# Three images of a conv-and-attention kernel: the cast after gelu set ahead of the exponentials, two low halves side by side, and input differences earlier

## What is computed

```python
perceived = conv_general_dilated(x, w_perc, padding='SAME', feature_group_count=Cc) + b_perc
hid = gelu(einsum('bphw,dp->bdhw', perceived, w_up1) + b_up1)
dx = einsum('bdhw,cd->bchw', hid, w_up2) + b_up2
h_new = transpose(x + dx)
qkv = einsum('bhwc,dc->bhwd', h_new, w_qkv) + b_qkv
scores = stack([(q * kp[shifted by dy, dx]).sum(-1) for dy, dx in _POS]) * scale
out = sum(softmax(scores)[i] * vp[shifted by dy, dx] for i in range(9))
return h_new + out
```

## Time and profile before

| what | value |
|---|---|
| median of 3 runs | 404.14 us (403.94 to 404.82) |
| the profiled execution's own time | 405.43 us |
| its span, first to last instruction | 403.1 us |
| TensorE busy | 386.1 us (96%) |
| TensorE weight loads | 362.9 us (90%) |
| VectorE busy | 340.5 us (84%) |
| ScalarE busy | 320.6 us (80%) |
| GpSimd busy | 177.4 us (44%) |
| mean granted TensorE clock | 0.990 |

### The profile page before, as it was taken

How to read it: one execution, slowest core, us unless ns; L and a number is a source line. 1 busy time by engine, 2 the same in 40 slices (tenths; PEclk the granted TensorE clock), 3 DMA queues, 4 the chain that set the end, 5 groups by cost and what they waited for, 6 DMA issues and landing times.

```text
span 403.1 us, 10500 instructions
## 1 busy us (share of the span) xinstructions
PE 386.1 (96%) x3674; PEld 362.9 (90%) x3674; DVE 340.5 (84%) x922; ACT 320.6 (80%) x710; POOL 177.4 (44%) x156
## 2 busy tenths in 40 slices
PE   6999975999999999999999999999999999999994
PEld 5999964998999999999999999999999999999874
DVE  5999975798898888888898888889888888886785
ACT  7635568789797997979798897979799797978873
POOL 6785164362626354351636354351636345032110
PEclk9999996999999999999999999999999999999999
DMA  7420300204013050504013050503104030301003
GB/s 232 167 65 2 120 0 18 101 2 146 28 55 116 2 172 1 169 0 131 38 34 135 0 169 0 169 0 104 65 12 157 0 104 2 104 2 54 3 37 120
DMA packets 11513, 28.57 MB, mean 71 GB/s; under 512 B 2400, under 2 KB 3296, under 8 KB 11488
## 3 DMA queue, kind: packets, MB, share of 16 engines
q1 hardware_dynamic: 11200, 28.21, 20.6%
q10 hardware_dynamic: 288, 0.05, 0.1%
HBM read 19.86 MB, written 8.39 MB: 70 GB/s over the span
## 4 chain that ended last, share of the span: by engine, by line
PE 73%; DVE 4%; issue 1%; POOL 0%; DVEq 0%; ACT 0%
PE m_ps L469 39%; PE s_ps L594 8%; PE work L524 8%; PE work L568 6%; PE s_ps L577 5%; PE s_ps L563 2%; PE s_ps L560 1%; PE s_ps L561 1%; PE work L594 1%; DVE t L946 1%; PE work L547 0%; DVE o_sb L1120 0%; PE m_ps L606 0%; DVE ptc L1111 0%; DVE pt L1126 0%
## 5 line engine op out<-in xcount | busy, mean ns | idle before, releaser
L469 PE MATMUL m_ps<-thi,whi 128*128 128x256 f32 x558 | 159.7, 286 | 0.7 <-DVE ru_sb L1034 0.4
L469 PE MATMUL m_ps<-thi,wlo 128*128 128x256 f32 x558 | 156.2, 280 | 0.0
L469 PE MATMUL m_ps<-tlo,whi 128*128 128x256 f32 x558 | 155.0, 278 | 0.0
L469 PEld LDWEIGHTS m_ps<-thi,whi 128*128 128x128 f32 x558 | 105.7, 189 | 4.0 <-issue 1.0
L469 PEld LDWEIGHTS m_ps<-tlo,whi 128*128 128x128 f32 x558 | 106.5, 191 | 0.7
L469 PEld LDWEIGHTS m_ps<-thi,wlo 128*128 128x128 f32 x558 | 105.6, 189 | 0.0
L1345 POOL TENSOR_TENSOR hid_lo<-hid,hid_hi 128x1024 fp32r<-128x1024 f32 x30 | 72.4, 2412 | 24.9 <-ACT hid_hi L726 20.4
L781 ACT COPY pt<-ptc 32x256 f32<-32x256 f32 (+3 forms) x186 | 73.0, 393 | 5.5 <-DVE ptc L1111 1.0
L1322 POOL TENSOR_TENSOR fc<-xp 128x512 f32<-128x512 f32 x16 | 21.6, 1347 | 110.1 <-DVE tlo L953 106.7
L716 ACT ACTIVATE hid<-y,b1eff 128x1024 f32<-128x1024 f32 x31 | 35.6, 1150 | 36.5 <-DVE y L1057 26.7
L795 ACT ACTIVATE p_sb<-p_sb,negmax 128x101 f32<-128x101 f32 x128 | 46.8, 369 | 7.0 <-DVE negmax L1092 7.0
(11 more groups left out here) (157 smaller groups left out, 787.5 us busy)
## 6 DMA issues: line engine op xcount, KB each, us to landing
xp<-x_planes SPq DMA_DIRECT2D x16, 640.0 KB, 5.2
xr<-x_rows SPq DMA_DIRECT2D x16, 512.0 KB, 4.0
out<-o_sb SPq DMA_DIRECT2D x28, 256.0 KB, 4.1
out<-y SPq DMA_DIRECT2D x3, 256.0 KB, 2.4
w1T<-w SPq DMA_DIRECT2D x1, 384.0 KB, 3.0
out<-y SPq DMA_DIRECT2D x2, 128.0 KB, 2.5
w2T<-w SPq DMA_DIRECT2D x1, 128.0 KB, 4.4
wqk_in<-w_qk SPq DMA_DIRECT2D x1, 128.0 KB, 4.3
```

The lines of the kernel that those rows point to most:

```text
L469: last = pe.matmul(bank[:, col + first:col + end], a[:, j, dy, half * P:(half + 1) * P], c[:, par, T_PLACE[j], first + by:end + by], start ...
```

## The change

In passes 1 to 3 it reorders instructions on ScalarE, VectorE and GpSimd; pass 3 gets an order of its own. `high_hid(n-1, 1)` and `take_m13(n, 0)` stand ahead of the exponentials in pass 1, and `high_hid` directly behind its gelu in pass 3. On GpSimd the differences of image 3 no longer wait for `low_t` of image 2; a wait for `combine_y` of image 1 stands behind them; and `low_hid(1, 1)` comes directly behind `low_hid(1, 0)`, ahead of the normalisations. VectorE makes the sums for image 3 and `combine(2, 0)` before the transposes of pass 1. Some of the placing copies stand later. In pass 3 VectorE makes `sum_h` and `low_h` before `transform`. At the start one of four fill-in matmuls is gone and `transform_ab(0, 0)` stands one instruction later. No arithmetic is changed.

```diff
--- before.py
+++ after.py
@@ -452,7 +452,7 @@
                 pe.wait_ge(bq_wide_done, 1)
                 pe.matmul(work[:, 2, 2 * P + 2:2 * P + 3], bq_wide[:, :], bqk[:, 1:2], start=True,
                           stop=True).then_inc(wt_ready, 1)
-                for _ in range(4):
+                for _ in range(3):
                     last = pe.matmul(m_ps[:, 2, S:CH], w1T[:, 0, 0:P], w1T[:, 0, 0:S], start=True, stop=True)
                 last.then_inc(warm_done, 1)
 
@@ -864,25 +864,44 @@
                     gelu(1, 0)
                     high_hid(1, 0)
                     gelu(1, 1)
+                    high_hid(1, 1)
+                    take_m13(2, 0)
                     for i in range(T):
                         exp(1, i)
                     prime_gelu()
                     return
                 if is_image(n, 2):
-                    high_hid(1, 1)
-                    take_m13(2, 0)
-                    place_p(2, 0, (0, 1, 2))
                     for c in range(NCH):
                         high_h(2, 1, c)
-                    place_p(2, 0, (3,))
+                    place_p(2, 0, (0, 1))
                     for c in range(NCH):
                         take_q(2, c)
                     high_t(3, 1)
                     gelu(2, 0)
                     take_m13(2, 1)
                     high_hid(2, 0)
+                    place_p(2, 0, (2, 3))
                     for i in range(T):
                         exp(2, i)
+                    prime_gelu()
+                    return
+                if is_image(n, 3):
+                    gelu(2, 1)
+                    high_hid(2, 1)
+                    take_m13(3, 0)
+                    place_p(3, 1, (0, 1))
+                    for c in range(NCH):
+                        high_h(3, 0, c)
+                    place_p(3, 1, (2,))
+                    for c in range(NCH):
+                        take_q(3, c)
+                    place_p(3, 1, (3,))
+                    high_t(4, 0)
+                    gelu(3, 0)
+                    take_m13(3, 1)
+                    high_hid(3, 0)
+                    for i in range(T):
+                        exp(3, i)
                     prime_gelu()
                     return
                 if attn:
@@ -988,8 +1007,8 @@
                         nc.vector.scalar_tensor_tensor(out=to[:, dy, :], in0=w1T[:, m, :],
                                                        scalar=wg[:, m, dy, i:i + 1], in1=acc[i][:, dy, :],
                                                        op0=ALU.mult, op1=ALU.add).then_inc(acc_done, 1)
-                    if k == 1 and m == 1:
-                        transform_ab(0, 0)
+                        if k == 1 and m == 2 and dy == 0:
+                            transform_ab(0, 0)
             transform(0, 0)
             dve.wait_ge(weights_in, 16 * N_W)
             nc.vector.tensor_copy(bq_wide[:, :], bqk[:, 0:1].to_broadcast([P, P])).then_inc(bq_wide_done, 1)
@@ -1235,14 +1254,15 @@
                     combine_y(1, 1)
                     finish_y(1, 1)
                     softmax_front(1, 1)
-                    for g in range(2):
-                        sums(1, g)
-                        turn_p(1, g)
+                    transform_ab(3, 1)
+                    sums(1, 0)
+                    combine(2, 0)
+                    turn_p(1, 0)
+                    sums(1, 1)
                     return
                 if is_image(n, 2):
-                    transform_ab(3, 1)
-                    combine(2, 0)
                     sum_h(2, 0)
+                    turn_p(1, 1)
                     low_h(2, 1)
                     transform(3, 1)
                     combine_y(2, 0)
@@ -1250,12 +1270,32 @@
                     low_t(3, 1)
                     softmax_front(2, 0)
                     combine(2, 1)
-                    sums(2, 0)
                     combine_y(2, 1)
                     finish_y(2, 1)
+                    sums(2, 0)
                     turn_p(2, 0)
                     sums(2, 1)
                     turn_p(2, 1)
+                    return
+                if is_image(n, 3):
+                    transform_ab(4, 0)
+                    combine(3, 0)
+                    for g in range(2):
+                        add_h(3, 0, g)
+                    sum_h(3, 1)
+                    low_h(3, 0)
+                    transform(4, 0)
+                    combine_y(3, 0)
+                    finish_y(3, 0)
+                    low_t(4, 0)
+                    softmax_front(3, 1)
+                    sums(3, 0)
+                    combine(3, 1)
+                    turn_p(3, 0)
+                    sums(3, 1)
+                    combine_y(3, 1)
+                    turn_p(3, 1)
+                    finish_y(3, 1)
                     return
                 if more:
                     transform_ab(n + 1, 1 - par)
@@ -1380,7 +1420,15 @@
                 if is_image(n, 1):
                     low_hid(0, 1)
                     sums_ab(2)
-                else:
+                    differences(3, 1)
+                    pool.wait_ge(y_part_done, 16)
+                    low_hid(1, 0)
+                    low_hid(1, 1)
+                    normalise(1, 0)
+                    sums_ab(3)
+                    normalise(1, 1)
+                    return
+                if not is_image(n, 2):
                     if more:
                         sums_ab(n + 1)
                     if attn:
```

## The result

The changed kernel takes 399.96 us (median of 4 runs, 399.87 to 401.2) against 404.45 us beside it: a ratio of 0.9897, 95% interval 0.9873 to 0.9920, or 4.5 us less. The one later series with the same kernel (e11) has 5.2 less: 399.92 against 405.15, ratio 0.9880, 0.9862 to 0.9897. The profiled execution's span went from 403.1 to 397.9, by 5.2. The spans of the kernel before vary more than those of the change: 30 later executions of it lie from 401.9 to 403.6, with their middle at 402.7, and 8 of the change from 397.8 to 398.1. The forecast was a gain of 5.2 and 398.9 us; its range was 395.6 to 401.7.

What follows compares the result with a forecast made beforehand. TensorE, 96% busy, was taken as the bound; removing its pass 2 waits promised about 10 us, ScalarE allowed 4.7, plus 0.5 slack: 5.2. Profiled 405.43 - 5.2 = 400.2, unprofiled 1.29 lower: 398.9 us, range 395.6 to 401.7.

Steps and rivals of the forecast that it cites:

- What bounds it: TensorE, 96% busy: gain lies in its pass 2 waits of 3.7 and 2.7 us and the low clock behind them.
- the clock term: Pass 2, behind the second wait: TensorE's clock at its lower level until 70.90 us, costing 2.3 us.
- Differences of image 3: GpSimd, no longer waiting for low_t of image 2: y of image 1 complete at 52.9 us, not 54.3.
- the collision with `low_t`: VectorE's low_t of image 2 meets GpSimd's last difference and ends 0 to 0.8 us later; 0.7 taken.
- Cast ahead of the exponentials: ScalarE, pass 1: exponentials still start at 56.95; pass 2's second dense layer loses both waits, ending at 58.9, not 67.3.
- ScalarE's stream: Passes 1 to 3: ScalarE cannot follow TensorE's gain of about 10 us; exponentials of pass 3 at 96.85, gain 4.7.
- the least time: ScalarE needs at least 37.7 us between exponentials of passes 1 and 3, which cannot start before 94.6: gain 7.0.
- From there to TensorE: Behind pass 3's exponentials: old order, 0.5 us of slack at h_lo, so TensorE at most 5.2 us earlier.
- The sum from TensorE's side: Cross-check on TensorE: 10.9 us of waits and low clock gone, 5.75 of new waits in passes 2 to 4, net 5.15.
- The first: Rival: other engines keep up better, ScalarE reaching its 7.0 us and TensorE 7.5 to 10; 395.6 us, chance 0.14.
- The second: Rival: clock falls again behind new waits of 0.85 to 1.65 us, 2.3 each; 401.2 to 403.5 us, chance 0.10.
- The third: Rival: new VectorE and GpSimd collision in passes from 4 on, 0.66 us in each of 12; 406.8 us, chance 0.04.

Runs made afterwards that it cites:

- e11: The changed kernel itself timed again, nothing edited, on one chip with other kernels: median 399.92 us, ratio 0.9880 to the kernel before.
- e2: The changed kernel with the exponentials of pass 1 and the second table load ahead of the cast and the m13 copy again: median 404.91 us.
- e4: The kernel before, with 14 and 10 fill-in matmuls in the two waits of pass 2's second dense layer: median 402.65 us, ratio 0.9941.
- e1: The changed kernel, but the differences of image 3 wait for low_t of image 2 again: median 401.91 us.
- e3: The changed kernel with pass 3 on ScalarE and VectorE in the common order of passes 4 and on: median 398.13 us, ratio 0.9832 to the kernel before.
- e7: The changed kernel with the old start, four fill-in matmuls and transform_ab(0, 0) where it was: median 399.89 us.
- e5: On top of e3, GpSimd in pass 3 runs low_hid(2, 1) ahead of the sums of image 4: median 398.69 us.
- e8: On top of e3, VectorE makes low_t of image 2 in two pieces, the second behind finish_y of image 1: median 397.48 us.

## Why the prediction was right

*What bounds it.* The two waits and the low clock were there as read. e2 brings the first wait and the low clock back by one edit, and the whole time with them; e4 measures the clock term: 2.1 for 2.3.

*Differences of image 3.* `fc` at 46.6 as said, y complete at 52.7 for 52.9. The bound on the collision with `low_t` was 0 to 0.8, 0.7 taken; it was 2.50 - 1.82 = 0.68. e1 shows that this step is worth 1.6 us at the end.

*Cast ahead of the exponentials.* Exponentials at 56.87 for 56.95; the layer of pass 2 without a wait from 56.1 to 59.0.

*ScalarE's stream.* This step carried the number: a gain of about 10 us at TensorE in pass 2 had to shrink to what ScalarE could follow. Its new idle times were forecast as 1.35 and 0.65, and were 1.5 and 0.6. The cast of `hid_hi(2, 1)` ended at 80.7, not 81.2, and the exponentials of pass 3 came at 96.44, not 96.85, 5.15 us earlier instead of 4.7. Without the two waits ScalarE spent 37.4 us between the exponentials (96.44 - 56.87 - 1.54 - 0.60). The forecast had 37.7 as the least time, and 0.25 for hand-overs on top. So the least time was no bound: in e3 the same exponentials lie 37.1 apart (93.90 - 56.80), 0.3 of it waiting, and start ahead of the 94.6 that the forecast called the earliest. It was added up from instructions that had partly stood behind waits, and such pairs get shorter when the wait goes, as e3 shows.

*From there to TensorE.* The first matmul that needs the low part started at 119.63, now:

```profile
113.55 0.47 PE L560 MATMUL s_ps<-h_hi,wqk_hi 128*128 128x512 f32 x1 [0.91 <-ACT h_hi L804]
...
114.27 0.51 PE L563 MATMUL s_ps<-h_lo,wqk_hi 128*128 128x512 f32 x1
```

5.36 us earlier, for 5.2; 0.09 of it is the earlier start of that execution. Of the 5.15 at the exponentials 0.2 went again before the gelu (4.9), and the slack of 0.5 added to it.

*The sum from TensorE's side* was less good. The new waits were forecast as 5.75 and are 4.4 on the list (0.2, 0.8, 0.7, 1.8, 0.9). By this sum the net would be 6.5, not 5.4. Where the other 1.1 us went is open; time lost in restarts behind waits is not on the list and was not measured.

*How good the agreement is.* That 5.2 stands against 5.2 in the spans is in part luck. The cast and the exponentials came 0.4 earlier than said, and half of that went again before the gelu; and the kernel before varies by 1.7 us from execution to execution. In device time the first series gave 4.5, and 398.9 was 1.1 too low. The profiled execution took 401.2, not 400.2: outside its span it spent 3.3 us, where the one of before had spent 2.3.

*Rivals.* The first (others keep up better) did not happen in this kernel, but e3 goes most of the way to it, with a span 7.7 us under the one before: leave pass 3 alone. The second was half right: the clock does fall behind a wait of 1.8 us in e1 and e2, and the mean clock of the changed kernel's own runs is 0.994 to 1.000. Its price of 2.3 was wrong, because another wait stands behind it and takes the loss up: over those mean clocks the spans of the change stay within 397.8 to 398.1. The third did not appear: behind the two waits of pass 4, TensorE's list has nothing up to the last attention.

## What to carry to other kernels

When a long wait of the bottleneck engine goes, ask next which engine had been idle because of it, and how much work that engine has to do without a pause: that sum says how much of the wait can be won; the wait alone promised about 10 us here, and 5.2 came. It is an estimate and no bound, since instructions that stood behind waits can get shorter. Then put no instruction of that engine behind an input that comes late; in pass 3 an order that served TensorE's next operand left ScalarE idle, and the kernel was 2.5 us faster without it. And where VectorE and GpSimd block each other, an instruction moved by a microsecond on one has to be checked against what the other runs just then: e5 lost 1.1 us to that, and e8 all that it had won.

## What the runs showed of the hardware

The clock can fall behind a wait of 1.8 us: in the profiles of e1 and e2 it was down at 0.50 within 1.5 us of the end of such a wait, in those of the change, e7 and e11, with the same wait of 1.8, it stayed at 1.00. What decides between the two is open here.

One small VectorE operation can be held up until a long GpSimd operation ends. In e8 the piece of `low_t` started at 52.17, while `hid_lo` ran from 51.72 to 54.13, and ended at 54.68: 2.51 us in place of 0.68. The Trainium skill, "SBUF — State Buffer", "SBUF: two separate sides", calls the port pair of the two an exclusive lock, held for the whole instruction, that a VectorE operation with two SBUF inputs has to take. The traces agree: the masked maxima and `combine`, with one operand in PSUM, kept their times of 0.26 and 0.68 us beside `hid_lo` in the kernel before.
